# Edge passes of a graph network: products four pairs ahead in four PSUM banks, sums added six tiles behind

## The reference

```python
for l in range(L):                       # L = 5
    xl = h @ W[l] + b[l]
    ee = edge_attr @ We[l] + be[l]       # edge_attr: 53125 x 128, We: 128 x 256
    msg = norm * jax.nn.relu(xl[row] + ee)
    agg = jnp.zeros_like(xl).at[col].add(msg)
    conv = agg + jax.nn.relu(xl + root[l]) / deg[:, None]
    ...                                  # batch norm over the nodes, ReLU, residual
```

## Time and profile before

| what | value |
|---|---|
| runs | 5602.98, 5607.82, 5611.37 us; median 5607.82 |
| the profiled execution | 5605.48 us, span 5603.7 us |
| busy in the span | PE 4159.1, PEld 3397.2, DVE 2968.8, ACT 2264.5, POOL 2962.8 us |
| mean granted TensorE clock | 0.897 of full speed |
| the five passes over the edges | 652.8, 652.9, 655.3, 653.0, 654.3 us |

### The profile page before, as it was taken

One profiled execution on the slowest core, in us unless ns is written; L12 is line 12 of the kernel. 1 busy time (PEld: TensorE's weight loads), 2 busy tenths in 40 slices (PEclk: granted clock), 3 DMA queues, 4 the chain that ended last, 5 costly groups with the idle time before them and its releaser, 6 DMA issues. The chain is left out here.

```text
span 5603.7 us, 96035 instructions
## 1 busy us (share of the span) xinstructions
PE 4159.1 (74%) x21956; PEld 3397.2 (61%) x21957; DVE 2968.8 (53%) x7177; ACT 2264.5 (40%) x4904; POOL 2962.8 (53%) x3202
## 2 busy tenths in 40 slices
PE   6888828779996777767777677776777767777588
PEld 4555517668885665656666566665656656666455
DVE  5555576652224555555555555555555555555634
ACT  2111136512223444444444444444444444444311
POOL 3666629623333666646666466664666646666142
PEclk8999959879998999989999899898999989999689
DMA  6666638536664444434444344443444434444332
GB/s 206 211 211 210 213 97 222 152 117 182 184 182 127 126 126 129 127 108 127 126 129 127 107 125 126 126 128 105 129 127 126 126 107 130 125 126 127 102 123 80
DMA packets 429338, 782.78 MB, mean 140 GB/s; under 512 B 212572, under 2 KB 269520, under 8 KB 412007
## 3 DMA queue, kind: packets, MB, share of 16 engines
q0 software_dynamic: 136704, 360.53, 23.3%
q1 hardware_dynamic: 281489, 402.18, 22.7%
q10 hardware_dynamic: 11094, 19.50, 1.2%
HBM read 669.16 MB, written 114.48 MB: 140 GB/s over the span
## 5 line engine op out<-in xcount | busy, mean ns | idle before, releaser
L2168 POOL DMA_INDIRECT g_g<-xl_table,g_idx x2080 | 1977.3, 951 | 1322.8 <-issue 556.4
L2202 PE MATMUL g_b<-g_we,g_ea 128*128 128x256 f32 x4160 | 1235.4, 424 | 600.5 <-DVE g_msg L2294 388.5
L2215 PE MATMUL g_b<-g_onehot,g_msg 128*128 128x128 f32 x8320 | 1258.5, 299 | 290.0 <-DVE agg L2307 119.3
L2215 PEld LDWEIGHTS g_b<-g_onehot,g_msg 128*128 128x128 f32 x8320 | 1167.4, 210 | 498.4 <-DVE agg L2307 323.3
L2294 DVE TENSOR_TENSOR g_msg<-g_g,g_b 128x512 f32<-128x512 f32 x1040 | 712.6, 685 | 1061.5 <-DMA g_g<-xl_table,g_idx 590.8
L2202 PEld LDWEIGHTS g_b<-g_we,g_ea 128*128 128x128 f32 x4160 | 776.8, 208 | 767.8 <-DVE g_msg L2294 444.5
L2307 DVE TENSOR_TENSOR agg<-agg,g_b 128x256 f32 x2080 | 864.4, 416 | 418.4 <-issue 167.7
L2258 ACT ACTIVATE g_away<-iota_row,dst_rel 128x128 f32<-128x128 f32 x1040 | 416.5, 400 | 1294.5 <-DMA g_g<-xl_table,g_idx 1127.9
L2276 ACT ACTIVATE g_msg<-g_msg 128x512 f32<-128x512 f32 x1040 | 645.9, 621 | 283.6 <-DVE g_msg L2294 213.6
L544 PE MATMUL sc_pe_h<-ae_h_rows,sc_onehot 128*128 x1664 | 467.3, 428 | 107.2 <-DVE sc_prod L649 103.1
L512 POOL DMA_INDIRECT sc_g<-h_table,sc_idx x416 | 404.6, 973 | 235.5 <-issue 104.6
(11 more groups left out here) (316 smaller groups left out, 3483.1 us busy)
## 6 DMA issues: line engine op xcount, KB each, us to landing
g_ea<-in_ea SPq DMA_DIRECT2D x260, 512.0 KB
ex_w<-in_f_w SPq DMA_DIRECT2D x80, 1024.0 KB
e_rows<-sc_g SPq DMA_DIRECT2D x52, 1088.0 KB
at_g<-e_rows SPq DMA_DIRECT2D x104, 544.0 KB, 4.5
g_g<-xl_table,g_idx POOLq DMA_INDIRECT x2080
xl_table<-g_rows SPq DMA_DIRECT2D x25, 640.0 KB, 3.8
sc_rel<-rel_row ACTq DMA_DIRECT2D x52, 256.0 KB
sc_g<-h_table,sc_idx POOLq DMA_INDIRECT x416
```

The source lines that it names most:

```text
L2168: nc.gpsimd.indirect_dma_start(out=g.g[:, j, :], out_offset=None, in_=k.xl_table[:, :], in_offset=bass.IndirectOffsetOnAxis(ap=g.idx[:, q, ...
L2202: last = nc.tensor.matmul(ep[u % EB][:, i * D:(i + 1) * D], g.ea[:, q, (at + i) * P:(at + i + 1) * P], g.we[:], start=True, stop=True)
L2215: last = nc.tensor.matmul(ps[u % (SB // 2)][:, at:at + P], g.msg[:, j, b * P:(b + 1) * P], g.onehot[:, j, :], start=True, stop=True)
```

## The change

- `EB` goes from 2 to 4: products are issued four pairs ahead, in four banks. The bank of the root product goes to this: `rp` is now bank 1 of the four.
- The root product therefore waits until DVE has used the products of pair 1, and PE issues products 5 and 6 only after ACT has read it, both behind sums 2. ACT reads it one pair earlier, ahead of the ReLU of pair 2.
- `LAG` goes from 4 to 6 tiles, in the passes and in the attention sums.
- SP issues the features of a half before it waits for the gathers of that half and issues the row numbers.

```diff
-LAG = 4
+LAG = 6
...
-    EB, SB = 2, 8
+    EB, SB = 4, 8
     START_AT = BODY - LAG
-    ep, ps, rp = g.banks[0:EB], g.banks[EB:EB + SB // 2], g.banks[EB + SB // 2]
+    NODE_SLOT = 1
+    ep, ps = g.banks[0:EB], g.banks[EB:EB + SB // 2]
+    rp = ep[NODE_SLOT]
...
             for q in range(2):
 
+                sp.wait_ge(g.product, used[q])
+                load_features(q, at[q][1])
                 for j in range(q * HALF, q * HALF + HALF):
                     sp.wait_ge(g.src_in[j], landed)
                 load_rows(q, at[q][0])
-                sp.wait_ge(g.product, used[q])
-                load_features(q, at[q][1])
...
             pe.wait_ge(g.rooted, it * K + K)
+            pe.wait_ge(g.raw, it * (BODY // 2) + NODE_SLOT + 1 + EB)
...
             for u in range(BODY // 2):
 
-                if u + 2 < BODY // 2:
-                    products(it, u + 2)
+                if u == NODE_SLOT:
+                    sums(it, u)
+                    node_tile(it)
+                    continue
+                if u == NODE_SLOT + 1:
+                    sums(it, u)
+                    pe.wait_ge(g.rooted, it * K + 2 * K)
+                    products(it, u - 1 + EB)
+                    products(it, u + EB)
+                    continue
+                if u + EB < BODY // 2:
+                    products(it, u + EB)
                 elif not final:
-                    products(it + 1, u + 2 - BODY // 2)
+                    products(it + 1, u + EB - BODY // 2)
                 sums(it, u)
-                if u == 1:
-                    node_tile(it)
-
-        products(0, 0)
-        products(0, 1)
+
+        for u in range(EB):
+            products(0, u)
...
                 hot_tile(it, 2 * u + 1, seen)
-                if u == 3:
+                if u == NODE_SLOT + 1:
                     act.wait_ge(g.xlt_ready, it + 1)
```

## The result

The changed kernel takes 5962.09 us, median of four runs (5946.33 to 5990.39), against 5608.53 us for the kernel before beside it: a ratio of 1.064, 95% interval 1.062 to 1.0659. It is 6.4% slower; forecast were 5540 us and a range up to 5685. The profiled execution took 5946.33 us, its span is 5944.6 us, and the mean granted clock is 0.85, where it was 0.897.

The account below looks back on a forecast made before the run. The prediction took POOL's pauses for PE's held marks to bound the passes. From 5605.5 us it took 143 saved, 75 lost at the root step and 2 for trailing additions: 5540 us, own range 5450 to 5595, cases from 5385 to 5685.

Parts of the forecast that it names:

- What bounds the kernel: In the passes, POOL pauses for PE's completion reports (marks), held while gathers are in flight; 4.5 us a body.
- I take one more pair between stalls: POOL's stalls in the passes: 4.1 pairs between them instead of 3.1, from earlier products and lag six; 143 us saved.
- Rival 2: POOL's stalls are set by gathers in flight and the window of four alone: no change, 5605 us; chance 0.13.
- The root step: Root product in the ring, read before ReLU 2, delays sums 2 and pair 6's gather: 75 us lost, bounds 0 to 207.
- the two products ahead of sums 3 cost nothing beyond that: On PE, products 5 and 6 issued ahead of sums 3: 2 x 0.86 us within a pair's 3.1 us, no extra loss.
- a longer stall there lets everything else catch up: At ACT's root wait, a longer stall spares a later one, so half of 152 us was counted: 75 us.
- Lag 6: DVE adds sums six tiles behind, no longer blocked by their mark: at most 140.4 + 103.1 us of waits removed.
- The 2 us for the additions at the end of a pass: On DVE, two more additions trail each pass, half under the last sums: 5 x 0.4 = 2 us lost.
- the zero of the attention stage: In the attention stage's additions, the larger lag shifts only the loop's break: zero taken, bounds 0 and one more break.
- Features ahead of rows at zero: On SP, loading features before row numbers only shifts two loads a body: zero taken.
- Rival 3: ACT's wait for the root mark delays pair 6's gather: full price 152 to 207 us, half the gain, about 5660; chance 0.29.
- Rival 4: PE idles after the root product, then works in a lump; clock falls to a mean of 0.85: 5680 us; chance 0.05.

Follow-up runs that it names:

- before_gathers_free: The kernel before, with POOL's gathers waiting for its own gathers four pairs back instead of PE's sums, and fixed rows used by DVE and ACT; 6612.5 us.
- before_no_gathers: The kernel before, gathering only in the first body of each pass and reusing those rows in all other bodies; 4510.4 us.
- after_no_root: The changed kernel without the root product and without held products, four pairs ahead in every slot, ACT reading h instead; ratio 0.9978 to the kernel before.
- before_no_root: The kernel before without the root product, ACT reading h instead without a wait; ratio 0.9979 to the kernel before.
- own_bank_read_at_2: The changed kernel with lag 4, root product in its own bank, three sums banks, nothing held, read ahead of ReLU 2; ratio 1.0117 to the kernel before.
- own_bank_hold: own_bank_read_at_2 with PE also holding products 5 and 6 behind sums 2 until ACT has read the root product; ratio 1.0942 to the kernel before.
- after_hold_only: The changed kernel without the root product, ACT reading h, PE still holding products 5 and 6 behind sums 2 until ACT has read; ratio 0.9969.
- before: The kernel before the change, unmodified; 5608.53 us beside the changed kernel, 5654 to 5663 us beside the other runs of the ratio table.

## Why the prediction was wrong

The sum was 5605.5 - 143 + 75 + 2 = 5540; measured is +340 in the profiled execution. Step by step:

- **What bounds the kernel** was right. The passes, POOL's pauses and the marks that are held until POOL pauses are shown by `before_gathers_free` and `before_no_gathers`, with some marks that come out between gathers as well.
- **"I take one more pair between stalls", -143 us, failed.** It measured nothing: `after_no_root` and `before_no_root` differ by 0.01%, though the first has all that was to gain. POOL's waits add to 733 and 744 us. The step counted the pairs that are finished at a release; but the number of pauses doesn't hang on that, for the mark that POOL needs is itself held by the gathers before it. Even a window of six pairs left the pauses. Rival 2 said this, and its other half, that nothing else moves, was wrong.
- **The root step, +75 us, failed in size.** It has all of the loss, 341 us, four to five times the 75 and more than the upper bound of 207. The step had three errors. The queue behind ACT's wait (ReLU 2, sums 2, the gather of pair 6) was right, and this alone measured 2.2% or 1.2%, 123 or 66 us; there the estimate of 75 would have held for size. But "the two products ahead of sums 3 cost nothing beyond that" was wrong: sums 2 are late, so POOL already waits, and the products of three pairs (4.38 us in the timeline) stand between sums 2 and sums 3, on which the gather of pair 7 waits. The hold adds 8.2% at lag 4 (`own_bank_read_at_2` to `own_bank_hold`). And half the price was taken off because "a longer stall there lets everything else catch up"; in the changed kernel products 5 and 6 are what would catch up, and they are held. The wait was also longer than the 2.0 us counted: ACT waits for "remote" 90 times in place of 66, 4.6 us each.
- **Lag 6**, counted within the 143 us, was worth nothing in the kernel before (1.001). In the changed one it saves 2.3 points of what the hold costs (1.0874 to 1.064), which no term had. The 2 us for the additions at the end of a pass and the zero of the attention stage held as far as 0.1% can show.
- **Features ahead of rows at zero** held in the kernel before: 1.0004.
- **Rival 3** named the place (pair 6, over 250 us of root wait) and not the size: 5660 against 5962. Its price left out the lump. **Rival 4**, the clock: it did fall, to 0.85, and PE is busy 137 us longer in the passes. But `after_hold_only` ran at 0.86 and 0.9969, and four banks without the root product at 0.875 took no longer than two at 0.892 (`after_no_root`, `before_no_root`). The low clock is a part of the lump's 4.38 us, not a cause for itself; how many us of the loss it makes was not measured apart.

The hold and the late mark don't add, and this is the point that a sum over parts can't have: hold -0.3%, wait +1.2% with four ahead, together +9.4% (at lag 4; the hold alone was measured at lag 6 and without the root product).

No version that gathers all its rows beat the kernel before by more than about 0.3%, and those that came below it leave out the root product or the feature loads. Four pairs ahead with the root product in its own bank, read at pair 3, does as well as two (1.0011).

## What to carry to other kernels

Where a trace shows that marks come in an engine's pause, more buffers ahead need not buy anything (here they bought nothing), and a wait for such a mark is better put behind the work that the pausing engine needs. A shared buffer that holds other work back cost nothing here as long as nobody waited, and 3.6 us a body (8.2% of 5655 us, over 130 bodies) once it stood behind a late mark: price the two together, not each for itself. Before counting a hold as hidden, ask what is next in the in-order queue behind the held work (here sums 3 behind three pairs of products) and who waits for that.

## What the runs showed of the hardware

- Marks of PE can be held for many us while POOL issues gathers, and most of them come out in its pauses. In `before_gathers_free` ACT waited 121 times for "remote" at the root product, 1608.3 us, at most 32.3 us. In `before_no_gathers` DVE's waits for sums were 219.6 us in 375, at most 1.2 us.
- On one chip the scoring stage, which gathers, had no wait for "remote"; on the others such waits were 293 to 320 us there (`before`, `before_no_gathers`).
- Without gathers the passes ran at a granted clock of 0.99, with them at 0.91 to 0.93 in the kernel before.
- The same chip ran the kernel before in 4923.5 us, where others took 5608 to 5663; it was seen once.
